# All zero writes of the slots' buffer in the first block, and the bias loads of the second mixture on GpSimd's queue

## The chip, the cores and the metric

The kernel runs on one core of a Trainium2 chip. A core has five engines that run side by side, each with its own queue of instructions: TensorE (PE: matmuls, and PEld: loading their weights), VectorE (DVE), ScalarE (ACT), GpSimd (POOL) and SyncE (SP). They meet only through semaphores. DMA transfers are issued by SP, ACT or POOL and are then carried out by 16 DMA engines. The metric is the device time of one execution in microseconds.

## The reference

The reference takes `x` (16 batches of 128 tokens, 256 numbers each) and a context of the same shape through four layers. Each layer adds `tanh(g) * xattn(layernorm(x))` and then `tanh(g) * ffn(layernorm(x))`:

```
layer 0: xattn = a decayed sum of the context, projected;   ffn = one linear map
layer 1: xattn = attention over masked context;             ffn = 16 experts, 4 per token, and a shared one
layer 2: xattn = attention with 32 heads;                   ffn = 16 experts, 2 per token, 2 shared, with biases
layer 3: xattn = attention over channels with 8 heads;      ffn = 16 experts, 4 per token, and a shared one
routed = sum over e of comb[token, e] * down_e(act(gate_e(h)) * up_e(h))
```

## The kernel before

All tokens stay in on-chip memory as 16 tiles of 128 tokens. The program is a row of blocks. Within a block each engine has its own list of instructions, written by hand and released by semaphores; at its end each engine jumps to a common point and waits there for all five (`barrier_Pool_Activation_PE_DVE_SP`), and only then does any of them go on.

The first blocks are `setup_and_decay` (loads, constants, layer 0's first half), `linear` (layer 0's second half), `masked_attention` (layer 1's first half) and `mixture(1, ...)` (layer 1's experts, "the first mixture"). After these come `many_heads`, `mixture(2, ...)`, `channel_heads`, `mixture(3, ...)` and `combine_last`.

A mixture works on slots. Each of the 16 experts owns 2048 rows of a buffer in HBM, `slots_in`, of 264 numbers each. DVE works out for each token the row that it gets with each of its experts (`row_in`, L1868, L1869), in two groups of 8 tiles in the first mixture; POOL then scatters the tokens there by indirect DMA (L2053), 32 of them for each group. Meanwhile PE, ACT and DVE go through the shared expert: `shared_gate_up` (L2147, L2152) and `shared_down` (L2166, L2170), six steps for each pair of tiles. The first three pairs are written out one after the other, the next four are a loop. After that, SP loads the tiles of the routed experts from `slots_in`.

A tile of an expert may have rows that no token went to, so before the first scatter the whole of `slots_in` is filled with zeros. `write_zeros(eng, first, end)` issues one DMA for each expert from a cleared buffer `xs_wide` (cleared by POOL at L314), and POOL waits at L2048 until all 16 have landed. All are issued by SP: 5 in `linear`, 5 in `masked_attention` behind the small loads there, 6 at the start of the first mixture.

The small loads in `masked_attention` prepare biases of the second mixture: SP loads `l2_gub`, POOL splits it in three bf16 parts (L571, L574), SP writes these to HBM (`bias_rows`, L559), waits for them and reads them back as three rows of `gbias` (L562).

Of the kernel before, what the change touches and what calls it, by code (L numbers as in the profile page):

```python
# [27 lines left out]
NE = 16  # L28
# [99 lines left out]
def _build(nc, io, top):  # L128
# [5 lines left out]
    x = sb("x", [P, NB, D])  # L134
# [17 lines left out]
    xs_wide = sb("xs_wide", [P, 2, W])  # L152
# [8 lines left out]
    gbias = sb("gbias", [P, NE * 256], BF16)  # L161
# [15 lines left out]
    slots_in, slots_out, bias_rows = io["slots_in"], io["slots_out"], io["bias_rows"]  # L177
# [3 lines left out]
    ZEROS = NE  # L181
# [8 lines left out]
    def write_zeros(eng, first, end):  # L190
        of_block = slots_in.rearrange("(t p) d -> p t d", p=P)
        for e in range(first, end):
            eng.dma_start(of_block[:, e * NB:(e + 1) * NB, :], xs_wide[:, 0:1, :].broadcast_to([P, NB, W])
                          ).then_inc(zeroed, 16)
# [16 lines left out]
    def load_experts(eng, layer):  # L211
        gu, dn, _, _, shared_dn = moe_views(layer)
        eng.dma_start(gu.rearrange("p e c i -> p (e c i)"), io[f"l{layer}_gu"]).then_inc(moe_loaded[layer - 1], 16)
        eng.dma_start(dn, io[f"l{layer}_dn"]).then_inc(moe_loaded[layer - 1], 16)
        eng.dma_start(shared_dn, io[f"l{layer}_sdn"]).then_inc(moe_loaded[layer - 1], 16)
# [28 lines left out]
    def setup_and_decay(measure, root, stats_ready, rooted, zeroed):  # L244

        with ExitStack() as st:
# [1 line left out]
            x_in = [sem(f"x_in{i}") for i in range(4)]  # L248
            ctx_in = [sem(f"ctx_in{i}") for i in range(4)]
            (cleared, gates_ready, own, cw_ready, based, beta_added, sums_done, sumT_ready, in_done, inT_ready,  # L250
             s_done, s_copied, spread, summed, g_ready, x_ready, w_ready) = (
                sem(n) for n in ("cleared", "gates", "own", "cw", "based", "beta", "sums", "sumT", "in", "inT",
                                 "s", "sc", "spread", "summed", "g", "x", "w"))
            numbers_i = sb("numbers_i", [P, ROUTED], I32, st)
            lanes_i = sb("lanes_i", [P, 4], I32, st)
            base_i = sb("base_i", [P, NE], I32, st)
# [13 lines left out]
            w = small["l0_w"]  # L270
            block = st.enter_context(nc.Block())

            @block.sync
            def _(sp):
                for i in range(4):
                    sp.dma_start(x[:, quarter(i)], io["x"][:, quarter(i)]).then_inc(x_in[i], 16)
                for i in range(4):
                    sp.dma_start(ctx[:, quarter(i)], io["ctx"][:, quarter(i)]).then_inc(ctx_in[i], 16)
                sp.dma_start(ctxT[:], io["ctxT"]).then_inc(ctxT_loaded, 16)
                load_experts(sp, 1)  # L280

            @block.scalar
            def _(act):
# [15 lines left out]
            @block.gpsimd  # L299
            def _(pool):  # L300
                nc.gpsimd.memset(ident[:], 0.0).then_inc(cleared, 1)
                nc.gpsimd.memset(ones[:], 1.0).then_inc(cleared, 1)
                nc.gpsimd.memset(neg_half[:], -0.5).then_inc(cleared, 1)
                pool.iota(numbers_i[:], pattern=[[1, ROUTED]], base=0, channel_multiplier=0).then_inc(cleared, 1)
                pool.iota(lanes_i[:], pattern=[[0, 4]], base=1, channel_multiplier=1).then_inc(cleared, 1)
                pool.iota(base_i[:], pattern=[[NB * P, NE]], base=1, channel_multiplier=0).then_inc(cleared, 1)
                pool.iota(token_i[:], pattern=[[4 * P, NB], [1, 4]], base=-int(FAR), channel_multiplier=4
                          ).then_inc(cleared, 1)
                pool.iota(spare_i[:], pattern=[[P, 8]], base=4 * NB * P - int(FAR), channel_multiplier=1
                          ).then_inc(cleared, 1)  # L310
                pool.wait_ge(cleared, 8)
                nc.gpsimd.affine_select(out=ident[:], in_=ident[:], compare_op=ALU.not_equal, fill=1.0, base=0,
                                        pattern=[[-1, P]], channel_multiplier=1).then_inc(cleared, 1)
                nc.gpsimd.memset(xs_wide[:], 0.0)  # L314
                nc.gpsimd.tensor_copy(numbers[:], numbers_i[:])
                for i in range(4):
                    nc.gpsimd.tensor_scalar(lanes[:, i:i + 1], lanes_i[:, i:i + 1], TAG * i, None, ALU.add)
                nc.gpsimd.tensor_copy(expert_base[:], base_i[:])
                nc.gpsimd.tensor_copy(token_rows[:], token_i[:])
                nc.gpsimd.tensor_copy(spare_rows[:], spare_i[:])  # L320
                root(pool, 0)
                root(pool, 1)
                pool.wait_ge(own, 9)
                for b in range(NB):
                    pool.wait_ge(based, b + 1)
                    nc.gpsimd.tensor_tensor(x[:, b, :], x[:, b, :], gg[:, 1, :], ALU.add).then_inc(beta_added, 1)
                pool.wait_ge(w_ready, 1)
                for c in range(C):
                    nc.gpsimd.tensor_tensor(w[:, c, :], w[:, c, :], small["l0_scale"], ALU.mult)
                for b in range(NB):  # L330
                    pool.wait_ge(stats_ready, NB + b + 1)
                    nc.gpsimd.tensor_tensor(xn[:, b, :], xn[:, b, :], gg[:, 0, :], ALU.mult).then_inc(g_ready, 1)
                    if b == 8:
                        root(pool, 2)
                for i in (3, 4, 5):
                    root(pool, i)
# [111 lines left out]
    def linear(measure, root, stats_ready, rooted, kept, blocked):  # L448

        with ExitStack() as st:  # L450
# [3 lines left out]
            block = st.enter_context(nc.Block())  # L454
            XT, Y = bank[0:2], bank[2:6]

            @block.sync
            def _(sp):
                write_zeros(sp, 0, 5)

            @block.gpsimd
            def _(pool):
                for b in range(NB):
# [68 lines left out]
    def masked_attention(measure, root, stats_ready, rooted, kept, blocked):  # L532
        carve = carver(1)
        with ExitStack() as st:
# [10 lines left out]
            bias_raw = carve([P, NE * 2])  # L545
            bias_part = [carve([P, NE]).bitcast(BF16) for _ in range(3)]
# [4 lines left out]
            def there(b):  # L551
                return 0 <= b < NB

            @block.sync
            def _(sp):
                sp.dma_start(bias_raw, io["l2_gub"]).then_inc(b_in, 16)
                for i in range(3):
                    sp.wait_ge(b_parted, i + 1)
                    sp.dma_start(bias_rows[i].rearrange("(p j) -> p j", j=NE * 2), bias_part[i]).then_inc(b_out, 16)  # L559
                sp.wait_ge(b_out, 48)  # L560
                sp.wait_ge(b_parted, 7)
                sp.dma_start(gbias[0:3], bias_rows).then_inc(b_back, 16)  # L562
                write_zeros(sp, 5, 10)
                sp.wait_ge(b_back, 16)

            @block.gpsimd
            def _(pool):
                step = Chain(pool, b_own)
                pool.wait_ge(b_in, 16)
                for i in range(3):  # L570
                    nc.gpsimd.tensor_copy(bias_part[i], bias_raw).then_inc(b_parted, 1)  # L571
                    if i < 2:
                        pool.wait_ge(b_parted, i + 1)
                        step(nc.gpsimd.tensor_tensor(bias_raw, bias_raw, bias_part[i], ALU.subtract))  # L574
                nc.gpsimd.memset(gbias[:], 0.0).then_inc(b_parted, 1)
                nc.gpsimd.memset(three_ones[:], 0.0).then_inc(b_parted, 1)
                pool.wait_ge(b_parted, 5)
                nc.gpsimd.memset(three_ones[0:3], 1.0).then_inc(b_parted, 1)
                pool.wait_ge(b_parted, 6)
                pool.sem_inc(b_parted, 1)  # L580
                root(pool, 8)
                root(pool, 9)

            @block.tensor
            def _(pe):
# [1350 lines left out]
    def mixture(layer, rt, carve, t0, scattered, late=0):  # L1936
# [11 lines left out]
        with ExitStack() as st:  # L1948
# [113 lines left out]

            @block.sync
            def _(sp):
                if layer == 1:
                    write_zeros(sp, 10, ZEROS)
                held = sp.alloc_register(f"block{layer}")
                blocks = slots_in.rearrange("(b p) d -> p b d", p=P)

                def load(n):  # L2070
                    sp.reg_load(held, n.of(tile_block))
                    at = sp.snap(held, min_val=0, max_val=NE * NB - 1)
                    if n.j is not None:
                        sp.wait_ge(turned, n.count(1 - U))
                        sp.wait_ge(picked, n.count(1 - U))
                    sp.dma_start(xg[n.c % U], blocks[:, ds(at, 1)]).then_inc(loaded[n.c % U], 16)

                sp.wait_ge(tiles_listed, 1)
                sp.wait_ge(scattered, 16 * NB * k)
                for c in range(U):  # L2080
                    load(Tile(c))
                with sp.Fori(0, turns) as j:
                    for c in range(U, 2 * U):
                        load(Tile(c, j))
# [591 lines left out]
```

## Time and profile before

| | us |
|---|---|
| median of 3 runs | 1409.24 |
| lowest and highest | 1405.26, 1410.93 |
| the profiled execution | 1406.2 |
| its span | 1404.5 |
| start of the linear stage | 72.07 |
| start of the masked attention | 97.52 |
| start of the first mixture | 136.34 |
| first scatter | 187.38 |
| first routed tile loaded | 344.55 |

All times in the profile are from the span's start. Over the whole span PE is busy 79% and DVE 54%, but the first 136 us belong to other engines: PE is busy 33.15 us of the first 72. "PEq L246" and names like it are the common points at the ends of blocks: an engine that waits for one waits for the other engines to arrive.

### The profile page before, as it was taken

The page shows a single profiled execution, that of the slowest core. Times are in us where ns is not written, and L with a number is a line of the kernel's source. Part 1 is how long each engine was busy: PE and PEld are TensorE (multiplying, and loading weights), DVE is VectorE, ACT ScalarE, POOL GpSimd, SP SyncE. Part 2 cuts the span into 40 slices and gives each one's busy share as a digit, 9 for nine tenths or more (in the row PEclk, how much of TensorE's full clock was granted, in tenths as well). Part 3 has the DMA queues.
Part 4 walks back from the last instruction along what each step waited for, and adds up shares of the span by engine and source line. Part 5 has one row for each costly group of instructions (what it writes and reads, how often), then busy time and mean ns, then how long its engine had stood idle before and what let it go on. Part 6 is the DMA issues. An engine that isn't in the chain of part 4 may idle for free. (4 is left out here: it accounts for less than half of the span.)

```text
span 1404.5 us, 25581 instructions
## 1 busy us (share of the span) xinstructions
PE 1105.6 (79%) x7222; PEld 815.2 (58%) x7223; DVE 753.7 (54%) x2787; ACT 487.8 (35%) x1309; POOL 609.9 (43%) x961
## 2 busy tenths in 40 slices
PE   4476984399999996799997779958887756599980
PEld 4364863287777774466665567845554434478770
DVE  6857432013444444687862555557777554365557
ACT  0054210011333332266653124424764422144440
POOL 5552056600333334565552404545564554345560
PEclk9998896699999998699996999977998876899995
DMA  9598942200333333211500114540002311256547
GB/s 407 160 309 266 340 142 89 92 0 16 104 106 106 106 106 107 77 47 61 219 25 32 66 43 134 155 157 2 2 2 117 137 67 66 85 136 165 145 132 299
DMA packets 92302, 169.45 MB, mean 121 GB/s; under 512 B 11103, under 2 KB 70751, under 8 KB 91231
## 3 DMA queue, kind: packets, MB, share of 16 engines
q1 hardware_dynamic: 72825, 114.71, 26.2%
q0 software_dynamic: 17664, 48.91, 9.6%
q10 hardware_dynamic: 1728, 4.79, 0.9%
q8 instruction: 44, 0.72, 0.2%
q14 instruction: 41, 0.33, 0.1%
HBM read 82.75 MB, written 85.61 MB: 120 GB/s over the span
## 5 line engine op out<-in xcount | busy, mean ns | idle before, releaser
L2236 PE MATMUL bank<-weights,xT 128*128 x832 | 241.0, 412 | 0.8 <-ACT xT L2330 0.7
L2059 POOL DMA_INDIRECT slots_out<-weights,y_rows x128 | 123.2, 962 | 155.3 <-DVE y_rows L2501 81.8
L2059 POOL DMA_INDIRECT slots_out<-pack,y_rows x80 | 77.0, 962 | 199.4 <-DVE y_rows L2501 190.8
L2053 POOL DMA_INDIRECT slots_in<-xn_wide,row_in x110 | 106.4, 968 | 124.1 <-DMA slots_in<-xs_wide 50.2
L2236 PEld LDWEIGHTS bank<-weights,xT 128*128 128x128 f32 x832 | 142.4, 191 | 25.9 <-issue 2.2
L2147 PE MATMUL bank<-xT,weights 128*128 128x256 f32 x416 | 113.0, 420 | 20.3 <-ACT xT L2294 16.7
L2330 ACT COPY xT<-bank 128x256 f32<-128x256 f32 x208 | 77.5, 373 | 111.3 <-PE bank L2228 104.2
L1471 PE MATMUL bank<-ctx,weights 32*128 32x256 f32 x512 | 80.5, 461 | 37.5 <-DVE weights L1627 27.9
L2147 PEld LDWEIGHTS bank<-xT,weights 128*128 128x128 f32 x416 | 85.7, 211 | 40.1 <-ACT xT L2294 14.1
L2432 DVE TENSOR_TENSOR rows<-rows,bank 128x256 f32<-128x256 f32 (+1 forms) x56 | 22.5, 402 | 147.4 <-ACT rows L2306 105.7
L1544 ACT ACTIVATE weights<-bank 128x512 f32<-128x512 f32 x128 | 72.6, 597 | 79.0 <-PE bank L1479 60.7
L1627 DVE TENSOR_REDUCE weights<-bank 128x2 f32<-128x512 f32 x128 | 86.0, 682 | 21.1 <-PE bank L1471 16.2
L2166 PE MATMUL bank<-weights,rows 128*128 128x256 f32 x256 | 73.4, 404 | 28.1 <-issue 21.8
L2478 DVE TENSOR_TENSOR weights<-weights,bank 128x128 f32<-128x128 f32 x128 | 36.9, 288 | 92.8 <-ACT weights L2334 83.9
L2306 ACT ACTIVATE rows<-bank 128x256 f32<-128x256 f32 (+1 forms) x56 | 20.7, 370 | 185.7 <-PE bank L2147 97.1
L1471 PEld LDWEIGHTS bank<-ctx,weights 32*128 32x128 f32 x512 | 51.5, 216 | 54.2 <-issue 24.4
L2253 PE MATMUL bank<-weights,pack 88*128 x320 | 82.2, 379 | 0.0
L1479 PE MATMUL bank<-weights 32*128 32x256 f32 x512 | 78.9, 451 | 1.4 <-ACT weights L1544 1.4
L2253 PE MATMUL bank<-weights 128*128 x256 | 77.3, 385 | 0.8 <-ACT weights L2338 0.8
L2478 DVE TENSOR_TENSOR pack<-pack,bank 128x176 f32<-128x176 f32 x80 | 27.1, 338 | 92.5 <-ACT pack L2334 78.7
L971 ACT ACTIVATE weights<-bank 128x512 f32<-128x512 f32 x128 | 71.5, 605 | 12.2 <-PE bank L865 11.8
L2166 PEld LDWEIGHTS bank<-weights,rows 128*128 128x128 f32 x256 | 48.7, 201 | 42.4 <-issue 33.3
(432 smaller groups left out, 2479.7 us busy)
## 6 DMA issues: line engine op xcount, KB each, us to landing
slots_in<-xs_wide SPq DMA_DIRECT2D x16, 2112.0 KB, 18.9
weights<-slots_in SPq DMA_DIRECT2D x96, 132.0 KB
xs_wide<-slots_in SPq DMA_DIRECT2D x72, 132.0 KB
weights<-slots_out SPq DMA_DIRECT2D x17, 512.0 KB, 17.4
rows<-slots_out SPq DMA_DIRECT2D x16, 512.0 KB, 3.3
weights<-in_l_gu SPq DMA_DIRECT2D x1, 7040.0 KB
pack<-slots_in SPq DMA_DIRECT2D x40, 132.0 KB
weights<-in_l_gu SPq DMA_DIRECT2D x1, 4608.0 KB, 16.2
```

The source lines that it names most:

```text
L971: nc.scalar.activation(e[:, G * c + g].rearrange("p j q -> p (j q)"), S[g][:], ACT.Exp, scale=HD ** -0.5).then_inc(e_ready, 1)
L1471: last = nc.tensor.matmul(score_bank(N * bs + ns)[:, j * L:(j + 1) * L], xh[bs % 2][rows, j, qh * P:(qh + 1) * P], ctx[rows, bs, :], start ...
L1479: last = nc.tensor.matmul(key_bank(N * b + n)[:, j * L:(j + 1) * L], km[b % 2][rows, j, c * P:(c + 1) * P], xm[b % 2][rows, j, :], start=T ...
L1544: nc.scalar.activation(eT[:, n].rearrange("p j q -> p (j q)"), key_bank(t)[:], ACT.Exp, scale=HD ** -0.5).then_inc(e_ready, 1)
L1627: nc.vector.tensor_reduce(peak[b % 2][:, qh, at:at + step_j + 1:step_j], score_bank(s)[:].rearrange("p (j l) -> p j l", j=2), AX.X, ALU.ma ...
L2053: pool.indirect_dma_start(out=slots_in, in_=xn_wide[:, t, :], in_offset=None, out_offset=bass.IndirectOffsetOnAxis(ap=row_in[:, t, i:i + 1 ...
L2059: pool.indirect_dma_start(out=slots_out, in_=y[:, n % U, :], in_offset=None, out_offset=bass.IndirectOffsetOnAxis(ap=y_rows[:, n % U:n % U ...
L2147: last = nc.tensor.matmul(out[:, side * D:(side + 1) * D], shared_gu[:, c, at:at + P], xp[:, c, :], start=(c == 0), stop=(c == C - 1))
L2166: last = nc.tensor.matmul(s_Y[t % 2][:, 0:D], sh_h4[:, n % ring, u * P:(u + 1) * P], shared_dn[:, i, :], start=(i == 0), stop=(i == pieces ...
L2236: last = nc.tensor.matmul(out, xT[:, n.c % 2, c, :], flat(gu_w[:, ds(e, 1), c, :]), start=(c == 0), stop=(c == C - 1 and layer != 2))
L2253: last = nc.tensor.matmul(Y[n.c % 2][:, 0:D], hT[:, n.c % 2, i, :], flat(dn_w[:, ds(e, 1), i, :]), start=(i == 0), stop=(i == parts - 1))
L2330: nc.scalar.copy(flat(xT[:, n.c % 2]), XT[n.c % 2][:, 0:D]).then_inc(xT_ready, 1)
```

## The change

All 16 zero writes are now issued by SP in the first block, behind the loads of the first experts; SP waits on a new semaphore, `blank`, that POOL raises when `xs_wide` is cleared. SP has nothing left in `linear` and `masked_attention`, and its zeros in the first mixture are gone. The small bias loads and stores are issued by POOL in `masked_attention`, the three stores after all of its casts and memsets, and POOL waits for `gbias` at the end of its list. No arithmetic changes.

```diff
+                sp.wait_ge(blank, 1)
+                write_zeros(sp, 0, ZEROS)
...
-                nc.gpsimd.memset(xs_wide[:], 0.0)
+                nc.gpsimd.memset(xs_wide[:], 0.0).then_inc(blank, 1)
...
-            @block.sync
-            def _(sp):
-                write_zeros(sp, 0, 5)
...
-            @block.sync
-            def _(sp):
-                sp.dma_start(bias_raw, io["l2_gub"]).then_inc(b_in, 16)
-                for i in range(3):
-                    sp.wait_ge(b_parted, i + 1)
-                    sp.dma_start(bias_rows[i].rearrange("(p j) -> p j", j=NE * 2), bias_part[i]).then_inc(b_out, 16)
-                sp.wait_ge(b_out, 48)
-                sp.wait_ge(b_parted, 7)
-                sp.dma_start(gbias[0:3], bias_rows).then_inc(b_back, 16)
-                write_zeros(sp, 5, 10)
-                sp.wait_ge(b_back, 16)
...
                 step = Chain(pool, b_own)
+                pool.dma_start(bias_raw, io["l2_gub"]).then_inc(b_in, 16)
                 pool.wait_ge(b_in, 16)
...
-                pool.sem_inc(b_parted, 1)
+                for i in range(3):
+                    pool.dma_start(bias_rows[i].rearrange("(p j) -> p j", j=NE * 2), bias_part[i]).then_inc(b_out, 16)
+                pool.wait_ge(b_out, 48)
+                pool.dma_start(gbias[0:3], bias_rows).then_inc(b_back, 16)
                 root(pool, 8)
                 root(pool, 9)
+                pool.wait_ge(b_back, 16)
...
-                if layer == 1:
-                    write_zeros(sp, 10, ZEROS)
```

The lists of the engines show where the instructions now stand. First SP before, from the start of the program to the first mixture; the branches are the ends of blocks and the entries into the next, and the square brackets name what is waited for:

```order
5 L213 DMA weights<-in_l_gu 128x14080
6 L214 DMA weights<-in_l_dn 88x8192
7 L215 DMA weights<-in_l_sdn 128x1536
8 L246 UNCONDITIONAL_BRANCH
9 L457 UNCONDITIONAL_BRANCH [waits barrier_Pool_Activation_PE_DVE_SP_release]
10 L193 DMA slots_in<-xs_wide 128x16x264 x5
11 L450 UNCONDITIONAL_BRANCH
12 L554 UNCONDITIONAL_BRANCH [waits barrier_Pool_Activation_PE_DVE_SP_release]
16 L193 DMA slots_in<-xs_wide 128x16x264 x5
17 L534 UNCONDITIONAL_BRANCH [waits l1a_b_back]
18 L2063 UNCONDITIONAL_BRANCH [waits barrier_Pool_Activation_PE_DVE_SP_release]
19 L193 DMA slots_in<-xs_wide 128x16x264 x6
```

The same place of SP in the changed kernel:

```order
5 L213 DMA weights<-in_l_gu 128x14080
6 L214 DMA weights<-in_l_dn 88x8192
7 L215 DMA weights<-in_l_sdn 128x1536
8 L193 DMA slots_in<-xs_wide 128x16x264 [waits l0a_blank]
9 L193 DMA slots_in<-xs_wide 128x16x264 x15
10 L246 UNCONDITIONAL_BRANCH
11 L2054 UNCONDITIONAL_BRANCH [waits barrier_Pool_Activation_PE_DVE_SP_release]
```

The sixteen writes stand ahead of SP's branch to the end of the first block (L246), where it met the other engines after the loads before. Then POOL in `masked_attention`, before:

```order
49 L571 CAST pack<-pack 128x32
54 L575 MEMSET gbias 128x4096
55 L576 MEMSET three_ones 128x128
56 L578 MEMSET three_ones 3x128
57 L2589 TENSOR_TENSOR rstd<-var,neg_half 128x8
58 L2591 TENSOR_TENSOR offset<-nmean,rstd 128x8
```

and in the changed kernel:

```order
49 L555 DMA pack<-in_l_gub 128x32
50 L558 CAST pack<-pack 128x32
55 L562 MEMSET gbias 128x4096
56 L563 MEMSET three_ones 128x128
57 L565 MEMSET three_ones 3x128
58 L568 DMA bias_rows<-pack 128x32 x3
59 L570 DMA gbias<-bias_rows 3x4096
60 L2578 TENSOR_TENSOR rstd<-var,neg_half 128x8
61 L2580 TENSOR_TENSOR offset<-nmean,rstd 128x8
```

Five DMAs have come onto POOL's list: one ahead of its first cast, four between its last memset and the root of the first half of the tiles.

## Rows read from the trace of the kernel before

**Rows 1.** The page: the span, and the DMA issues (KB each, us to landing).

```profile
span 1404.5 us, 25581 instructions
...
slots_in<-xs_wide SPq DMA_DIRECT2D x16, 2112.0 KB, 18.9
```

**Rows 2.** Waits of all engines, 0 to 320 us: total, times, longest us.

```profile
POOL slots_in L2053 <- DMA slots_in<-xs_wide: 50.2, 1, 50.2
...
ACT xn_wide L497 <- PEq L246: 34.3, 1, 34.3
...
POOL pack L571 <- DMA pack<-in_l_gub: 9.5, 1, 9.5
```

**Rows 3.** Timeline of SP's DMA issues, from several windows: start us, us, what, xcount.

```profile
9.49 1.38 SPq L215 DMA_DIRECT2D weights<-in_l_sdn  x1
...
72.07 2.40 SPq L193 DMA_DIRECT2D slots_in<-xs_wide  x2
72.07 21.73 SPq L193 DMA_DIRECT2D slots_in<-xs_wide  x5
74.52 6.19 SPq L193 DMA_DIRECT2D slots_in<-xs_wide  x1
...
112.37 60.77 SPq L193 DMA_DIRECT2D slots_in<-xs_wide  x11
114.78 6.85 SPq L193 DMA_DIRECT2D slots_in<-xs_wide  x1
128.49 6.63 SPq L193 DMA_DIRECT2D slots_in<-xs_wide  x1
```

**Rows 4.** SP's own waits.

```profile
SPq L246 <- PEq L246: 61.0, 1, 61.0
...
SPq L450 <- PEq L450: 3.5, 1, 3.5
...
SPq L534 <- PEq L534: 0.2, 1, 0.2
```

**Rows 5.** Windows: stretch us, length, busy of PE, PEld, DVE, ACT, POOL, PEclk, DMA share, GB/s.

```profile
46.00:50.00 4.00, 4.00 (x11) 3.08 (x10) 3.90 (x15) 0.00 (x0) 2.46 (x4) 1.00 0.48 98
60.00:64.00 4.00, 0.00 (x0) 0.00 (x0) 3.90 (x16) 0.00 (x0) 0.51 (x1) 1.00 0.40 123
64.00:68.00 4.00, 0.00 (x0) 0.00 (x0) 4.00 (x12) 0.00 (x0) 1.53 (x2) 1.00 0.00 0
187.40:280.00 92.60, 44.56 (x177) 31.56 (x176) 16.22 (x81) 5.87 (x16) 61.91 (x64) 0.70 0.26 94
280.00:344.50 64.50, 63.99 (x331) 52.43 (x332) 19.57 (x51) 12.11 (x32) 0.00 (x0) 0.95 0.00 0
```

**Rows 6.** Timeline at block ends: POOL's last work, SP's first in the mixture.

```profile
71.55 0.20 POOL L2591 TENSOR_TENSOR offset<-nmean,rstd 128x8 f32<-128x8 f32 x1
...
132.28 0.20 POOL L2591 TENSOR_TENSOR offset<-nmean,rstd 128x8 f32<-128x8 f32 x1
...
136.34 4.89 SPq L193 DMA_DIRECT2D slots_in<-xs_wide  x1
```

**Rows 7.** Timeline of POOL: clearing the zero buffer, and the masked attention.

```profile
2.38 0.53 POOL L314 MEMSET xs_wide<- 128x528 f32 x1
...
111.75 0.20 POOL L578 MEMSET three_ones<- 3x128 bf16 x1
119.61 1.64 POOL L2589 TENSOR_TENSOR rstd<-var,neg_half 128x8 f32<-128x8 f32 x1 [7.66 <-DVE var L2583]
```

**Rows 8.** Timeline of DVE, POOL and PE in the first mixture: [idle before <-releaser].

```profile
177.56 0.17 DVE L1869 TENSOR_SCALAR xn_wide<-best 128x32 f32<-128x32 f32 x1
187.38 1.24 POOL L2053 DMA_INDIRECT slots_in<-xn_wide,row_in  x1 [50.23 <-DMA slots_in<-xs_wide]
203.26 0.31 PE L2152 MATMUL bank<-xT,weights 128*64 128x128 f32 x1 [0.42 <-issue]
234.19 0.96 POOL L2053 DMA_INDIRECT slots_in<-xn_wide,row_in  x1 [6.30 <-DVE xn_wide L1869]
```

More of the change, by code:

```diff
@@ L250, in setup_and_decay @@
             (cleared, gates_ready, own, cw_ready, based, beta_added, sums_done, sumT_ready, in_done, inT_ready,
-             s_done, s_copied, spread, summed, g_ready, x_ready, w_ready) = (
+             s_done, s_copied, spread, summed, g_ready, x_ready, w_ready, blank) = (
                 sem(n) for n in ("cleared", "gates", "own", "cw", "based", "beta", "sums", "sumT", "in", "inT",
-                                 "s", "sc", "spread", "summed", "g", "x", "w"))
+                                 "s", "sc", "spread", "summed", "g", "x", "w", "blank"))
             numbers_i = sb("numbers_i", [P, ROUTED], I32, st)
```

## The prediction

> **What bounds the kernel now.** I read the page first, then the waits of all engines up to 320 us, the timeline of SyncE (SP) with one window per DMA issue, SP's own waits, the timelines on both sides of each block boundary, and the table of windows for DMA traffic. The chain of waits on the page covers the last 34 us only, so it says nothing here; the front of the kernel is a row of closed blocks and has to be read block by block.
>
> The wait that the change goes for is in [rows 2]: POOL sits 50.2 us in the first mixture until the zeros have landed. It is real, but four fifths of it are hidden. The row numbers that POOL needs are placed by DVE at 177.56 + 0.17 = 177.7 us, and the first scatter starts at 187.38 [rows 8]. Only 9.7 us of the 50.2 are owed to the zeros; for the rest the data was not there.
>
> What the zeros cost SP is the other reading. There are 16 writes of 2112 KB [rows 1]. The first two of a series are issued in 2.40 us together, but the third takes 6.19 us, and in the second series the third takes 6.85 [rows 3]. SP can run about two writes ahead and then stands in the issue until an older one has landed. In the long series of eleven, the third ends at 114.78 + 6.85 = 121.63 and the last at 112.37 + 60.77 = 173.14, so eight issues take 51.5 us, 6.44 each [rows 3]; that is 336 GB/s. After SP's last issue, 14.2 us pass until POOL sees everything landed (187.38 - 173.14): 2.2 writes. So SP is free when write number n - 2 has landed.
>
> Each block ends in a meeting of all five engines, SP included: SP waited there 61.0 us at the end of the first block, where it had finished at 9.49 + 1.38 = 10.9 us, 3.5 us at the end of the linear stage, and 0.2 us at the end of the attention, where it came last [rows 4]. At that last one POOL, the last engine with work of its own, had finished at 132.28 + 0.20 = 132.48, SP ended its fifth write at 128.49 + 6.63 = 135.12, and everybody started the mixture at 136.34 [rows 3, 6]. There SP already holds back the whole core.
>
> **The change, part by part.**
>
> (a) All 16 writes in the first block. The loads ahead of them on the same queue are in transit until about 63.5 us: the window 60 to 64 still shows a share of 0.40, 64 to 68 shows 0.00 [rows 5]. Behind them write 14 lands at 63.5 + 14 x 6.44 = 153.7 us, and that is when SP is through with the sixteenth. A block boundary costs 0.3 us after the last engine (POOL ends at 71.75, SP goes on at 72.07 [rows 3, 6]). So the linear stage starts at 154.0 instead of 72.07: +81.9 us. Everything in the first block of the other engines (to 71.75, POOL [rows 6]) lies under it, and so does any disturbance there.
> Bounds. From below: in the later part of the loads the DMA share is far under 1 (0.48 at 46 to 50, 0.40 at 60 to 64 [rows 5]). If the writes could run as if alone from about 44 us on, shortly ahead of that first window, write 14 would land at 44 + 90 = 134 and the term is +62. Against it: a write is complete only when every engine's part is, and the parts queue behind the loads. From above, 6.85 per write [rows 3] gives 63.5 + 95.9 + 0.3 = 159.7, +87.6. I take +81.9, nearest to the row of the series of eleven.
>
> (b) The waits on the new semaphore. The memset of the zero buffer ends at 2.38 + 0.53 = 2.9 us [rows 7], SP comes there at 10.9. Nothing.
>
> (c) The linear stage, now without five issues. SP ended at 72.07 + 21.73 = 93.8 and waited 3.5 us for the others [rows 3, 4], so it did not close this stage. The last two writes are under way in its first 13 us, where five were before. 0, with 1 us to either side for what the transfers disturb: PE's part of it ran beside them before.
>
> (d) The attention, now without SP. The mixture starts 1.22 us after the last engine (136.34 - 135.12). With POOL last, at 132.48, it is 133.70: -2.6 us. A bound on the other side: POOL now issues the five small DMAs and waits for them. It waited 9.5 us for the bias before, with zero writes still ahead of it [rows 2]; its casts and memsets end at 111.95, and its next work, the root of the first half, comes 7.7 us later [rows 7]. The first indirect DMA keeps POOL 1.24 us [rows 8], so four more after 111.95 are 5.0 us and fit. Those roots are wanted only in the mixture, and the second one stands at 132.48, 20.5 us after 111.95. Cost 0: the four issues and two further waits of 7.7 each still fit under the second root (5.0 + 15.4 = 20.4). At worst each of the two is as long as the old 9.5 and 3.5 us are added. I take -2.6.
>
> (e) The scatters. With the zeros landed by 167 us and the mixture starting at 215.6, the wait of 50.2 becomes 40.5 and the first scatter starts 9.7 us earlier within the stage. I value it at 0. In this stretch PE is held up: from 187.4 to 280 it is busy 44.6 of 92.6 us [rows 5], and the matmuls of L2152 come singly with gaps put down to "issue" and not to any engine [rows 8]. They start 15.9 us after the first burst of 32 scatters does (203.26 - 187.38). The second burst, at 234.19, has waited 6.3 us for DVE's rows, which depend on PE's steps [rows 8]. If the first burst starts 9.7 us earlier, PE gets its held-up time earlier and has 9.7 us more work left before it; the second burst comes at the same moment of the stage. After 280 the stage is bound by PE (63.99 of 64.5 us [rows 5]). Bounds: -9.7 (the whole head start passes through) and +24 (one more held-up stretch, half of 48.0, if the earlier scatters meet more new code).
>
> Sum: +81.9 - 2.6 + 0 = +79.3. On the profiled execution's 1406.2 us (span 1404.5 [rows 1]) this is 1485.5. The median of the runs shown, 1409.24, lies 3.0 above it; I put the forecast at 1486, the sum rounded up with a small part of that.
>
> **The rivals.**
> R1, faster: SP's issues do not hold the other engines, or are not held themselves. Then the linear stage starts at 72 as before, -2.6 at the attention and 0 to -9.7 in the mixture: 1394 to 1404. The trace speaks against it twice: the length of the issues 3 to 11 and SP's place at 135.12. It decides from the point where SP leaves the first block before 71.75.
> The Trainium skill ("Perfetto Trace Analysis", DMA Instruction — HWDGE) says that an issue's row ends when its descriptors are made and holds no data movement. Taken alone it would have 16 issues of 1.2 us, SP free at 30 us, and this rival's time. The trace agrees for the first two writes, 2.40 us for both, and not for the third at 6.19.
> R2, slower by less: the zeros fill the gaps of the loads from 44 us on. 1406.2 + 62 - 2.6 = 1466, down to 1456 with the scatters' 9.7.
> R3: the forecast's delay, but the scatters' head start passes through: 1485.5 - 9.7 = 1476.
> R4: the forecast's delay and one more stretch in which PE is held up: 1485.5 + 24 = 1509.
> R5: the change doesn't do what it says, POOL still waits for zeros. With the last write landing at 63.5 + 16 x 6.44 = 166.5 us and the row numbers due at 177.7 + 79.3 = 257.0, there are 90 us between; I give it no chance.
>
> **How the numbers follow.** Forecast (1479 to 1493) 0.52; R2 0.14; R3 0.18; R4 0.07; R1 0.04; something else 0.05, nearly all of it slower. The likeliest is 1486. The range 1456 to 1504 leaves out R1, most of R4 and part of the last. A change within 0.5% (7 us, about what a measurement can tell from none) would need R1 with no gain in the mixture. Faster 0.03, within 0.5% 0.02, slower 0.95.
>
> **What would show it.** In the profile after: SP's sixteen writes in one piece from 10.9 us to about 153.7, most of them 6.4 us long; the other engines' waits for the end of the first block (34.3 us for ACT before [rows 2]) at about 116 for ACT; DVE idle from 70 to 154; the first matmul of the linear stage at about 154.7; the mixture's first work at about 215.6; POOL's wait before the first scatter on DVE's row numbers and no longer on the zeros; the rest of the program as before, later by 79. Nothing downstream can take it back: each block starts only when all engines meet. I am wrong if SP leaves the first block well before 150 us, or if the stretch from the linear stage's start to the first mixture's start (64.3 us before) is not about 61.6, or if the first mixture changes its length by more than 10 us.

## The result and the profile after

The changed kernel takes 1490.08 us (median of 4 runs, 1484.4 to 1492.34) against 1410.09 for the kernel before on the same chip (4 runs): 1.0562 times as long, 95% interval 1.0514 to 1.061. The forecast was 1486 with a range of 1456 to 1504. The profiled execution took 1492.09 us, with a span of 1490.4, which is 85.9 more than before's 1404.5.

The page of the changed kernel, with its span, its DMA share in 40 slices, what the DMA engines moved, and the scatters of the rows:

```profile
span 1490.4 us, 25579 instructions
DMA  9899400211013333331150012443000511146547
GB/s 406 248 341 342 126 2 1 105 63 65 0 48 107 107 107 107 93 102 58 46 218 23 30 66 64 135 129 131 2 2 2 217 67 66 66 122 163 156 124 289
L2044 POOL DMA_INDIRECT slots_in<-xn_wide,row_in x110 | 106.5, 969 | 126.3 <-DVE xn_wide L1860 80.4
```

The DMA engines are now 80% busy or more in each of the first four slices (149 us), and in the next three (4, 0, 0), where the kernel before still wrote zeros, they have little to do. The scatters wait for DVE and no longer for zeros.

SP's issues in the changed kernel, one window per issue (columns: start, length, engine's queue, line, operation, out<-in; adjacent issues of a line are joined, so the windows overlap):

```profile
9.81 1.39 SPq L215 DMA_DIRECT2D weights<-in_l_sdn  x1
11.24 53.05 SPq L193 DMA_DIRECT2D slots_in<-xs_wide  x2
...
12.54 51.75 SPq L193 DMA_DIRECT2D slots_in<-xs_wide  x1
...
64.34 18.66 SPq L193 DMA_DIRECT2D slots_in<-xs_wide  x3
...
146.69 6.24 SPq L193 DMA_DIRECT2D slots_in<-xs_wide  x1
```

The first write is issued in 1.3 us. The second stands in its issue for 51.75 us, until 64.29: that is when the loads ahead are through, forecast as 63.5. The other fourteen take until 146.69 + 6.24 = 152.93, so (152.93 - 64.34) / 14 = 6.33 us each, where 6.44 was forecast from [rows 3].

What the other engines waited for in the changed kernel up to 405 us (columns: engine, line, releaser: us in total, times, longest), then SP's own waits:

```profile
ACT xn_wide L495 <- PEq L246: 115.4, 1, 115.4
...
DVE kept L512 <- PEq L246: 83.2, 1, 83.2
...
POOL slots_in L2044 <- DVE xn_wide L1860: 60.2, 2, 43.9
```

```profile
SPq L532 <- PEq L532: 35.6, 1, 35.6
SPq L452 <- PEq L452: 25.3, 1, 25.3
...
SPq L246 <- PEq L246: 0.2, 1, 0.2
```

SP's wait of 61.0 us at the end of the first block [rows 4] has become 0.2: SP is now the last to come there. In its place it waits through the whole linear stage (25.3) and the attention (35.6), where it has no work left. ACT's wait for that meeting went from 34.3 [rows 2] to 115.4; DVE waits 83.2.

The changed kernel's timeline at the starts of the linear stage, the attention and the first mixture, and at both bursts of scatters (columns: start, length, engine, line, operation, tiles, [idle before <-releaser]):

```profile
153.35 1.59 ACT L495 ACTIVATE xn_wide<-x,offset,rstd 128x256 f32<-128x256 f32 x3 [115.45 <-PEq L246]
...
154.00 1.18 PE L477 MATMUL bank<-ident,xn_wide 128*128 128x128 f32 x4 [102.03 <-ACT xn_wide L495]
...
187.26 1.65 POOL L568 DMA_DIRECT2D bias_rows<-pack  x3 [0.31 <-POOL three_ones L565]
190.32 0.57 POOL L570 DMA_DIRECT2D gbias<-bias_rows  x1 [1.42 <-DMA bias_rows<-pack]
200.77 1.67 POOL L2578 TENSOR_TENSOR rstd<-var,neg_half 128x8 f32<-128x8 f32 x1 [9.88 <-DVE var L2572]
...
215.19 0.21 POOL L1922 MEMSET pack<- 128x128 f32 x1 [1.54 <-POOLq L2555]
215.43 0.38 DVE L2342 MEMSET pack<- 128x384 f32 x1 [3.78 <-PEq L2555]
...
259.89 1.13 POOL L2044 DMA_INDIRECT slots_in<-xn_wide,row_in  x1 [43.91 <-DVE xn_wide L1860]
...
316.56 0.96 POOL L2044 DMA_INDIRECT slots_in<-xn_wide,row_in  x1 [16.25 <-DVE xn_wide L1860]
```

The linear stage starts at 153.35 instead of 72.07, the first mixture at 215.19 instead of 136.34. Between the two lie 61.8 us, 64.3 before. The scatters wait for DVE's row numbers and no longer for zeros. DVE's first work of the mixture came 78.8 us later than before (215.43 against 136.59), and there the loss is complete. The five stretches from there (the first mixture, `many_heads`, the second mixture, `channel_heads`, and the third mixture with the end) changed by +3.6, -0.9, +3.2, -4.8 and +6.0 us. The profiles of five later runs on chips of the same speed, with the same code behind that point, scatter about as much: their first mixture took 416.8 to 419.9 us (before 416.5, changed 420.1), the last stretch 232.9 to 242.9. The medians are 80.0 us apart, close to the 78.8.

### The profile page after: what moved, and what is told of

It is laid out like the page before. It is cut to its first block and busy times, and to the rows that moved or that the text cites. A ratio compares the mean times of both kernels' runs of the same rounds, so it can differ in the third digit from the quotient of the medians.

```text
span 1490.4 us, 25579 instructions
## 1 busy us (share of the span) xinstructions
PE 1103.6 (74%) x7222; PEld 813.6 (55%) x7223; DVE 754.1 (51%) x2787; ACT 486.9 (33%) x1309; POOL 613.1 (41%) x966
## 5 line engine op out<-in xcount | busy, mean ns | idle before, releaser
L2136 PE MATMUL bank<-xT,weights 128*128 128x256 f32 x416 | 117.7, 432 | 25.2 <-issue 23.1
L2136 PEld LDWEIGHTS bank<-xT,weights 128*128 128x128 f32 x416 | 88.7, 218 | 43.9 <-issue 25.2
L1462 PE MATMUL bank<-ctx,weights 32*128 32x256 f32 x512 | 76.9, 445 | 38.7 <-DVE weights L1618 26.4
L477 PE MATMUL bank<-ident,xn_wide 128*128 128x128 f32 x32 | 6.8, 303 | 102.0 <-ACT xn_wide L495 102.0
## 6 DMA issues: line engine op xcount, KB each, us to landing
weights<-in_l_gu SPq DMA_DIRECT2D x1, 4608.0 KB, 16.4
```

Of the source, the lines that this page charges most:

```text
L1462: last = nc.tensor.matmul(score_bank(N * bs + ns)[:, j * L:(j + 1) * L], xh[bs % 2][rows, j, qh * P:(qh + 1) * P], ctx[rows, bs, :], start ...
L2136: last = nc.tensor.matmul(out[:, side * D:(side + 1) * D], shared_gu[:, c, at:at + P], xp[:, c, :], start=(c == 0), stop=(c == C - 1))
```

## The experiments

Kernels of one set shared a chip with the kernel before. Its median was 1408.01 us in the first set (23 runs), 1274.83 in the second (7), 1274.32 in the third (21) and 1408.18 in the fourth (7). Each set had a chip of its own. The same kernel takes 9.5% less on those of the second and third set, called the faster chips below, so times are compared inside a set, or as microseconds added up to the first mixture. There the chips hardly differ: it starts at 136.59 us in before's profile and at 137.12 in a profile from the third set.

**First set: the two parts apart, and how many zeros.** `zeros_only` has all sixteen writes in the first block and leaves the small loads with SP (the edit against the kernel before).

```diff
 load_experts(sp, 1)
+sp.wait_ge(blank, 1)
+write_zeros(sp, 0, ZEROS)
...
-write_zeros(sp, 0, 5)        # linear
-write_zeros(sp, 5, 10)       # attention
-write_zeros(sp, 10, ZEROS)   # mixture
```

> The zeros' part of the change alone: all 16 writes in the first block, the bias loads stay with SP in the masked attention. Theory (SP can only run two writes ahead and every block ends when all engines have come, so SP's sixteen issues behind the loads hold the first block): the linear stage starts at 153 to 154 us, the mixture at about 215, and the time is that of the changed kernel within 3 us, +80 us on the kernel before. Rival (POOL's new small DMAs cost a part of the 80): this kernel would be visibly faster than the changed one, by 5 us or more.

Measured: 1488.14 us, 1.0574 times before (1.0518 to 1.063); linear stage at 153.98, mixture at 215.44. The writes alone make the whole loss, and POOL's small DMAs add nothing to it.

`bias_only` does the other half: the small loads go by POOL's queue and the zeros stay in their three blocks (0 to 5, 5 to 10, 10 to 16).

> The other part alone: the small loads on POOL's queue, the zeros stay 5, 5 and 6 with SP. Theory: SP now starts its five writes of the masked attention at 97.5 instead of 112.4 us and is done at about 124, before POOL's last root at 132.5, so the mixture starts at 133.7, 2.6 us earlier; the last zero lands at about 176 and POOL's wait for zeros shrinks to about 1 us. Whole time -2.6 us, if the scatters' head start is worth nothing; -12 us if the head start of 9 us passes through. Rival (POOL's own DMA chain closes the attention): no gain, or slower by 2 to 5.

Measured: 1406.97 us, 0.999 times before (0.9964 to 1.0016). The mixture starts at 134.84, 1.75 us earlier and not 2.6, and the first scatter at 180.84, still behind the zeros, by 2.2 us (DVE had the row numbers at 178.6):

```profile
180.84 1.13 POOL L2050 DMA_INDIRECT slots_in<-xn_wide,row_in  x1 [45.46 <-DMA slots_in<-xs_wide]
```

So this half costs nothing, and what it gains is inside the interval.

`eight_first` puts eight writes into the first block, four into the attention, four into the mixture; this edit and the next two are against the changed kernel.

```diff
-write_zeros(sp, 0, ZEROS)
+write_zeros(sp, 0, 8)        # first block
+write_zeros(sp, 8, 12)       # attention
+write_zeros(sp, 12, ZEROS)   # mixture
```

> Half the dose: 8 writes in the first block, 4 in the masked attention, 4 in the mixture; small loads on POOL's queue. Theory: SP leaves the first block when write 6 has landed, 63.5 + 6 x 6.44 = 102.1; the linear stage starts at 102.4, +30.3; the attention gives 2.6 back; whole time +28 us. If instead the delay were a fixed disturbance of mixed loads and zeros (no count of writes in it), it would stay near +80; if the writes could fill the gaps of the loads, the linear stage would start at about 83 and the time be +8.

Measured: 1435.09 us, 1.018 times before (1.0119 to 1.024). Linear stage at 102.53, mixture at 164.71. SP's last issues in this kernel's first block:

```profile
76.63 25.46 SPq L193 DMA_DIRECT2D slots_in<-xs_wide  x4
...
95.85 6.24 SPq L193 DMA_DIRECT2D slots_in<-xs_wide  x1
```

SP leaves at 102.09; landing of write 6 behind the loads is 63.5 + 6 x 6.44 = 102.1. The changed kernel, with eight writes more, leaves 50.84 us later (152.93), 6.36 for each. So each write beyond the number that fits costs one landing, 6.3 to 6.4 us.

`fitted` asks for as many as fit: three in the first block, four in the linear stage, five in the attention, four in the mixture, the small loads with POOL.

```diff
-write_zeros(sp, 0, ZEROS)
+write_zeros(sp, 0, 3)        # first block
+write_zeros(sp, 3, 7)        # linear
+write_zeros(sp, 7, 12)       # attention
+write_zeros(sp, 12, ZEROS)   # mixture
```

> The zeros spread as 3, 4, 5 and 4 over the first block, the linear stage, the masked attention and the mixture, so that SP should never be the last at a block's end; small loads on POOL's queue. Theory: with write k issued when write k-2 has landed and 6.44 us per write from 63.5 us on, SP leaves the first block at about 70, the linear stage at about 96 (POOL: 97.2) and the attention at about 128 (POOL: 132.5); stages start at 72.1, 97.5 and 133.7; all zeros are down at about 167, before the row numbers at 175. Whole time -2.6 us against the kernel before, up to -12 if the scatters' head start passes through. If the blocks do not wait for SP (rival R1), it is the same as the changed kernel in time, which stands at +80.

Measured: 1404.73 us, 0.9974 times before (0.9946 to 1.0002). SP's waits at the ends of the attention, the first block and the linear stage:

```profile
SPq L536 <- PEq L536: 3.9, 1, 3.9
...
SPq L246 <- PEq L246: 1.7, 1, 1.7
SPq L452 <- PEq L452: 1.3, 1, 1.3
```

SP is nowhere last any more, and the scatters wait for DVE alone (44.16 us, first one at 179.64 against 187.38). The 7.7 us are not in the whole: first tile 208.5 us after the mixture's start, 208.0 before. Its median is the lowest of the first set, 3.3 us under before's, and its interval still includes no change.

**Second set: the order, a second queue, late scatters.** `two_queues` gives half of the writes to ACT's queue, which has no large loads ahead.

```diff
-write_zeros(sp, 0, ZEROS)
+write_zeros(sp, 0, 8)
...
+act.wait_ge(blank, 1)
+write_zeros(act, 8, ZEROS)
```

> The changed kernel with the 16 writes of the first block shared: 8 issued by SP behind the loads, 8 by ScalarE's queue after its last work there (37.8 us). Theory with a limit of two writes ahead for each queue: the same bytes at the same rate, but four writes may be under way when both issuers are free, and ScalarE's writes may use what the loads leave from 42 us on: the linear stage starts at 130 to 136 us instead of 153, time +57 to +63 on the kernel before. If the two ahead are a limit of the core and not of a queue: 142 to 150. If a queue without loads ahead were free of back-pressure, ScalarE would leave early and SP's eight would set about 102 to 115.

Measured: 1343.52 us, 1.0543 times before (1.0522 to 1.0564); linear stage at 143.83 and not 130 to 136. Issues of this kernel's SP, then of its ACT:

```profile
12.65 54.63 SPq L193 DMA_DIRECT2D slots_in<-xs_wide  x1
...
67.32 25.06 SPq L193 DMA_DIRECT2D slots_in<-xs_wide  x2
...
118.32 25.07 SPq L193 DMA_DIRECT2D slots_in<-xs_wide  x2
```

```profile
38.10 39.80 ACTq L193 DMA_DIRECT2D slots_in<-xs_wide  x2
...
65.38 25.07 ACTq L193 DMA_DIRECT2D slots_in<-xs_wide  x2
...
116.38 25.09 ACTq L193 DMA_DIRECT2D slots_in<-xs_wide  x2
```

On each queue a write now takes 12.5 us, half the rate, so one lands every 6.3 us as before. If the second queue has a count of its own, two writes ahead, four fewer than sixteen have to be landed: 63.5 + 12 x 6.44 = 140.8. SP left at 118.32 + 25.07 = 143.39. The time alone does not decide, for 143.8 lies in the 142 to 150 that I expected from a limit of the whole core. The bytes decide. First this kernel from SP's leaving to the end of the zeros, then the changed kernel from its own (columns: stretch, its length, busy us and instructions of PE, PEld, DVE, ACT, POOL, granted clock, DMA share, GB/s):

```profile
143.39:165.50 22.11, 20.57 (x96) 16.59 (x96) 14.73 (x39) 13.79 (x32) 14.32 (x19) 1.00 0.87 270
152.93:166.00 13.07, 11.94 (x53) 9.54 (x54) 7.85 (x16) 9.21 (x21) 7.97 (x12) 1.00 0.81 255
```

That is 5.97 MB, 2.8 writes, still to be moved here, and 3.33 MB, 1.5 writes, in the changed kernel. Two writes ahead for the core would leave at most two; two for each queue can leave more. My expectation also assumed that ACT's writes would use the gaps between the loads. They hardly did: from 42 to 64 us the DMA engines moved 231 GB/s here and 195 in the changed kernel, over 22 us a third of a write more. ACT stood in its second issue from 38.10 to 65.35, as SP did in its own to 67.28. That also speaks against the rival in which zeros fill the gaps (R2).

`zeros_then_loads`, too, is edited from the changed kernel; it has the same sixteen writes ahead of the experts' loads instead of behind them.

```diff
-load_experts(sp, 1)
 sp.wait_ge(blank, 1)
 write_zeros(sp, 0, ZEROS)
+load_experts(sp, 1)
```

> The changed kernel with the loads of the first experts behind the 16 writes, not ahead. Theory: the writes start behind x, ctx and ctxT only, at about 20 us, so write 14 lands at about 110 and write 16 at 123; SP leaves with its last load between these, the linear stage starts at 108 to 125 us instead of 153, time +34 to +50 on the kernel before; the experts' loads then land at about 165, before the mixture needs them. If it was not the queue ahead of the writes that set the delay, nothing changes against the changed kernel (+80).

Measured: 1322.91 us, 1.0381 times before (1.036 to 1.0402); linear stage at 122.47. In this kernel SP issues:

```profile
5.48 108.88 SPq L193 DMA_DIRECT2D slots_in<-xs_wide  x16
114.40 6.74 SPq L213 DMA_DIRECT2D weights<-in_l_gu  x1
```

SP still has to see nearly all zeros landed, but no longer the loads: 30.9 us less than with the change (153.35). The bytes in this block are the same; what counts is which of them are still outstanding when SP may go.

`late_scatters` goes for term (e). Two theories of why PE is held up beside the scatters: A, the scatters themselves do it, so later scatters leave PE's early work alone; B, PE would be held up there anyway, by something of its own. The kernel is before's, with POOL held until PE has done 23 steps of its shared-expert work.

```diff
 pool.wait_ge(zeroed, 16 * ZEROS)
+pool.wait_ge(sh_used, 23)
```

> The kernel before, with POOL holding back the 64 scatters of the first mixture until PE has done 23 steps of the shared expert (it is then in the second round of its loop). It asks why the head start of the scatters was worth nothing. Theory A (scatters hold PE only where it comes to code for the first time): steps up to there run at full pace, PE is at step 24 at about 220 us instead of 280, the scatters run from 220 to about 303 under the loop, the first routed tile is loaded at about 305 to 325 instead of 344.5, time -20 to -40. Theory B (scatters hold PE whatever it does, by their traffic): PE is held up by the same 48 us later on, the first tile comes at 344 or later, time 0 to +20.

Measured: 1300.94 us, 1.021 times before (1.0193 to 1.0227); first scatter at 224.47. `fitted_late` has `fitted`'s writes and this wait.

> The zeros spread as 3, 4, 5 and 4, small loads on POOL's queue, and the scatters of the first mixture held back until PE's step 23. Gains should add: -2.6 us (start of the mixture) to what the held back scatters give alone: -23 to -43 us by theory A, -3 to +18 by theory B.

Measured: 1301.16 us, 1.0216 (1.0195 to 1.0236). Both lose 26 us, which is in the range of neither theory, and both ran on a faster chip, where the effect under study was not there. The third set shows that on another chip of that speed.

**Third set: another of the faster chips.** `before_again` is the kernel before, unchanged, for a profile on such a chip.

> The kernel before, unchanged. In one set of runs its median was 1408 us, in the other 1275 us, and in the second set the kernels with the changed front took 102 us from the first scatter to the first routed tile instead of 157 to 167. This run shows the profile of the kernel before on the chip of this set. If the holding up of PE while POOL scatters belongs to the chip, then here either PE is busy about 45 of 93 us in that stretch and the time is near 1408, or there are no such gaps and the time is near 1275. If it belongs to what the changed fronts do, this profile shows the gaps whatever the time.

Measured: 1274.59 us, 1.0006 (0.9996 to 1.0017). Its first 72 us and its 92.6 us after 187.4 (columns: stretch, its length, busy us and instructions of PE, PEld, DVE, ACT, POOL, granted clock, DMA share, GB/s):

```profile
0.00:72.00 72.00, 33.15 (x112) 27.02 (x113) 51.65 (x158) 2.95 (x7) 39.23 (x67) 1.00 0.77 276
...
187.40:280.00 92.60, 92.60 (x503) 76.47 (x502) 32.58 (x124) 20.20 (x50) 61.84 (x64) 1.00 0.26 94
```

In [rows 5] PE was busy 44.6 of the same 92.6 us at a granted clock of 0.70. Here PE gets through 503 matmuls instead of 177 beside the same 64 scatters of POOL, and is busy all the time. The first tile comes 147.3 us after the mixture's start, against 208.0.

`late_scatters_2` repeats `late_scatters` beside before_again.

> The kernel before with the first mixture's scatters held back until PE's step 23, once more. Where PE is held up while POOL scatters (time of the kernel before near 1408): theory A (only code that is new is held up) -20 to -40 us, theory B (everything is held up) 0 to +20. Where it is not (near 1275): +26 us as measured in the first set, since the scatters then end later than PE's own work.

Measured: 1301.45 us, 1.0217 (1.02 to 1.0234), as before. With PE never held up, scatters that start 37 us later only end later: the last one is issued at 304.89, and the first tile moves from 284.40 to 308.07. Which of A and B holds on the slower chips was not tried there and stays open.

`fitted_2` repeats `fitted`.

> The zeros spread as 3, 4, 5 and 4 with the small loads on POOL's queue, once more, to halve the uncertainty of its ratio (0.9974, 0.9946 to 1.0002). Theory: the mixture starts 2 us earlier; whole time -2 to -4 us, more (up to -10) where the scatters do not hold PE up.

Measured: 1273.4 us, 0.9992 (0.9983 to 1.0002). Its first scatter is at 178.70, behind DVE's numbers alone, 9.1 us earlier than before_again's 187.78; its first tile comes 146.9 us after the mixture's start, against 147.3. The head start is worth nothing here either. The gain of 0.9 us by the medians is under the 2 to 4 that I expected, and the interval includes no change.

**Fourth set.** `changed_again` is the changed kernel, meant for a faster chip.

> The changed kernel, unchanged, once more. The runs so far came from chips of two kinds: 1408 us and 1275 us for the kernel before. Theory: the delay is made of transfers and a block's end alone and is the same number of microseconds on either, +79 (linear stage at 153, mixture at 215), so near 1354 where the kernel before takes 1275, and near 1488 where it takes 1408. Rival: the delay grows with whatever makes the one kind of chip slower (10%), and is about 72 us on the faster kind.

Measured: 1488.94 us, 1.0573 (1.0502 to 1.0645), but on a chip on which before takes 1408.18. It repeats the result (linear stage at 153.50, mixture at 216.11) and does not answer the question. The change itself was never timed on a faster chip; two_queues (+68.7 us) and zeros_then_loads (+48.1) lost there what their mixtures' late starts say (+69.2 and +47.4 against before_again).

## Why the prediction was right

**(a), all writes in the first block: right.** Forecast +81.9, measured +81.3 (153.35 - 72.07). Each of its parts is in the profile: loads through at 64.29 for 63.5, 6.33 us per write for 6.44, SP away at 152.93 for 153.7, ACT's wait 115.4 for 116. The step "SP is free when write n - 2 has landed" gives SP's leaving to 1 us at n = 16 and n = 8, and with two for each queue to 2.6 us in two_queues. The prediction cited the Trainium skill ("Perfetto Trace Analysis", DMA Instruction — HWDGE) for a row that ends when the descriptors are made and holds no data movement. The first write agrees (1.3 us). The second write's row, 51.75 us, lasted until older transfers had moved; whether descriptors were still being made in it, no row shows.

**The lower bound of (a), R2: refuted.** The writes did move bytes in the gaps: the share at 46 to 50 us is 0.89 in the changed kernel, where [rows 5] has 0.48.

```profile
46.00:50.00 4.00, 4.00 (x10) 3.12 (x10) 3.86 (x15) 0.00 (x0) 2.44 (x4) 1.00 0.89 222
```

Yet the first issue that had to wait was released at 64.29. The gaps were also worth little: from 42 to 64 us the DMA engines moved 195 GB/s in the changed kernel and 150 before, over 22 us 1.0 MB or half a write more, where R2's 20 us would need three. My objection to R2, that a write is complete only when every engine's part is, fits this; no run shows it apart.

**(b), (c): right.** The new semaphore holds nothing. From the linear stage to the attention it is 25.3 us (153.35 to 178.70).

**(d), the attention without SP: right.** -2.4 us (61.84 against 64.27) for -2.6. Either half gives it alone: from ACT's first work in the attention to DVE's first in the mixture it is 39.0 us before, 36.3 in zeros_only, 36.8 in bias_only and 36.7 with both. POOL's chain of DMAs fits with room: three issues in a row take 1.65 us together and not 1.24 each, the wait behind them is 1.42 and not 7.7, and POOL then has 9.88 us of idle time before its first root at 200.77. The 3.5 us of the upper bound came nowhere near.

**(e), the scatters: the value right, the head start's size and the reason not.** The head start was 6.3 us and not 9.7: the scatter came 44.5 us after DVE's first work (259.89 - 215.43) where before had 50.8. The row numbers themselves came 2.4 us later in the stage (43.5 us into it, before 41.1), and before's scatters had waited for zeros until 50.8. The unchanged kernel in before_again has the numbers 2.8 us later as well, so this is not the change's doing. What differs is the granted clock (columns as for before_again), here in the changed kernel:

```profile
229.00:233.00 4.00, 3.97 (x10) 2.72 (x10) 0.42 (x3) 2.09 (x4) 0.00 (x0) 0.50 0.00 0
233.00:237.00 4.00, 3.57 (x10) 3.04 (x11) 1.90 (x8) 0.37 (x1) 0.00 (x0) 0.50 0.01 4
```

That is 13.6 to 21.6 us into the stage, granted 1.2 of 2.4 GHz. The kernel before, 13.4 to 21.4 us into its stage:

```profile
150.00:154.00 4.00, 3.61 (x10) 2.71 (x10) 0.73 (x3) 2.27 (x5) 0.00 (x0) 0.63 1.09 341
154.00:158.00 4.00, 3.41 (x21) 2.92 (x21) 2.72 (x17) 0.83 (x3) 0.00 (x0) 1.00 1.09 341
```

There the clock rises inside the first of the two windows and is full in the second, though PE had been busy about as much in both stages until then (11.4 of 13.6 us, before 11.2 of 13.4); why it rose earlier, the rows do not show. It goes with the row numbers in all fourteen profiles: they stand 41.1 to 41.6 us into the stage in the three where the clock had begun to rise by 18 us (before, late_scatters and late_scatters_2), and 43.5 to 43.9 in the eleven where it was still 0.50 at 20 us. The first tile then came 211.6 us after the mixture's start, 208.0 before: nothing of the head start arrived.

The reason that I gave was that PE is held up beside the scatters. In the changed kernel it is, from the first of them:

```profile
276.33 3.78 PE L2136 MATMUL bank<-xT,weights 128*128 128x256 f32 x8 [6.63 <-issue]
...
289.67 0.59 PE L2136 MATMUL bank<-xT,weights 128*128 128x256 f32 x1 [1.74 <-issue]
...
306.36 0.77 PE L2171 MATMUL bank<-pack 128*128 128x128 f32 x2 [14.00 <-issue]
```

```profile
266.20:358.80 92.60, 46.27 (x191) 34.31 (x190) 16.34 (x81) 6.78 (x17) 56.77 (x59) 0.69 0.24 88
```

The first row starts 16.4 us after the first scatter, 15.9 in [rows 8]; over 92.6 us PE is busy 46.3, before 44.6. So over the same part of the stage PE is held up about as much as before, and the second burst comes 101.1 us into the stage (97.6 before). But that is not what makes the head start worth nothing, for on the faster chips PE has no such gaps and it is worth nothing all the same. SP's last wait before it loads the first routed tile names the cause, in the kernel before, the changed kernel, before_again and late_scatters_2 (columns: who waits, for whom: us in total, times, longest):

```profile
SPq L2071 <- DVEq L2417: 67.8, 1, 67.8
SPq L2060 <- DVEq L2406: 68.0, 1, 68.0
SPq L2071 <- DVEq L2417: 13.4, 1, 13.4
SPq L2080 <- DMA slots_in<-xn_wide,row_in: 133.7, 1, 133.7
```

In the first three SP waits for DVE's list of the experts' tiles (`tiles_listed`), and the scatters are long done: the last one was issued 70.0 us before the first tile's load in the kernel before, 70.2 in the changed kernel, 15.6 in before_again. Only where they were held back until step 23 are they the last to come. So a head start of the scatters does not reach the first tile by itself on either kind of chip. On the slower ones it could still act through the time for which PE is held up, if that moved DVE's list, and no gain of that sort came. The trace of the kernel before had this wait, and the prediction does not use it: it argued a zero that was right from a step that does not decide it. In so far the zero was luck.

**R1, R3, R4, R5: refuted.** SP was held and held the others (R1). Zeros_only, the changed kernel and fitted show no head start in the time (R3), no second held-up stretch (R4). POOL does not wait for the zeros (R5). How little the wait of [rows 2] was worth, as (e) had it, shows best in fitted, which takes all of it away at no cost and is 3.3 us faster by its median, with an interval that includes no change.

## What to carry to other kernels

Before work is moved to a queue's front, count what is outstanding on that queue where its engine has to meet the others: an issue that stands still holds the meeting, and here each write beyond the third delayed every engine by 6.1 to 6.3 us (30.4 us for five, 81.3 for thirteen). The length of a wait is not its worth: of POOL's 50.2 us, four fifths were hidden by row numbers that were not there, and the rest by DVE's list of tiles, which came 70 us after the last scatter (15.6 in before_again). To value a head start, look up what ends the last wait of the work that it is to bring forward. Where a forecast rests on gaps that no engine explains, look at the same kernel on a second chip before building on them.

## What the runs showed of the hardware

- The unchanged kernel took 1408 us on two chips and 1274 on two others. The profiles of the two kinds are within 0.6 us of each other at the start of the first mixture. From the first scatter on PE was busy 44.6 of 92.6 us on the one kind (granted clock 0.70) and 92.6 on the other (1.00). The gaps are put down to "issue"; POOL issues indirect DMAs there on both. What causes them is open.
- A queue let its engine run about two writes of 2112 KB ahead. The count is per queue: with two queues 2.8 writes were still to be moved when SP left, with one 1.5, and each of the two ran at half the rate (12.5 us per write for 6.3). Behind large loads on the same queue the second write already stood (51.75 us).
- A small plain DMA issued by POOL kept it 0.55 us in a row of three, 0.57 and 0.82 alone; they had landed 1.42 and 1.6 us after the issue ended.
- The granted clock rose from 0.50 about 4 us earlier in three of fourteen profiles, with the same code in that part of the stage, and in these three DVE's row numbers came about 2.4 us earlier; before and before_again are the same kernel and stand on either side.
